# Keeping the last two tiles of each image in SBUF until their coefficients are known, instead of the last one

## What is computed

```python
g = _gn(x)                                   # group norm, 32 groups of 8 channels, no affine part
s = 0.5 * (abs(dx(g)) + abs(dy(g))) + 0.5 * abs(g)      # [-1,0,1] differences, zero padding
sp = mean of s over each 32 x 32 patch       # (4, 256, 64 patches)
ranks = argsort(argsort(-sp, axis=1), axis=1)
mask = ranks < 128                           # in each patch the 128 strongest of 256 channels
return x + g * mask
```

## Time and profile before

| | |
|---|---|
| median of 3 runs | 2076.13 us (2074.24 to 2077.39) |
| the profiled execution: its time | 2073.52 us |
| its span, first to last instruction | 2071.8 us |
| mean granted TensorE clock | 0.829 |
| busy share of the span | VectorE 76%, ScalarE 74%, TensorE 66%, GpSimd 64% |
| DMA traffic | 776.53 MB, mean 375 GB/s |
| HBM read and written | 507.51 MB and 268.44 MB |
| chain that ended last, largest shares | DMA 51%, ScalarE 15%, issue 10%, TensorE 8%, VectorE 8% |

### The profile page before, as it was taken

The page is one execution under the profiler, slowest core; times in us unless marked ns, Lnnn a source line. Parts: engine busy times, 40 slices in busy tenths (PEclk is TensorE's granted clock), DMA queues, the critical chain, the costliest instruction groups (busy, mean ns, idle before and its releaser), DMA issues.

```text
span 2071.8 us, 16156 instructions
## 1 busy us (share of the span) xinstructions
PE 1373.3 (66%) x3528; PEld 673.3 (33%) x3528; DVE 1571.7 (76%) x2160; ACT 1538.2 (74%) x2357; POOL 1321.6 (64%) x894
## 2 busy tenths in 40 slices
PE   5899899786787778676777778776777778300000
PEld 2444444343333334333333334333333334100000
DVE  7988888888777877799778887988778787861322
ACT  4999999897889888998798889997798889400000
POOL 7999899587677766578676667677676667300000
PEclk9999999888888888888888888898988888655555
DMA  6744555199999999999999999999999999699999
GB/s 251 337 183 199 206 243 213 61 369 433 430 429 432 432 434 428 388 370 434 426 431 431 434 429 432 394 395 424 429 432 432 434 428 378 289 420 430 432 430 389
DMA packets 41239, 776.53 MB, mean 375 GB/s; under 512 B 4576, under 2 KB 4576, under 8 KB 4576
## 3 DMA queue, kind: packets, MB, share of 16 engines
q1 hardware_dynamic: 41184, 775.96, 88.5%
HBM read 507.51 MB, written 268.44 MB: 375 GB/s over the span
## 4 chain that ended last, share of the span: by engine, by line
DMA 51%; ACT 15%; issue 10%; PE 8%; DVE 8%; DVEq 2%; POOL 2%; SPq 1%; ACTq 1%; POOLq 0%
DMA again<-in_x_dram 40%; ACT again L653 8%; DMA out_dram<-ring 7%; PE vertical L557 4%; DMA ring<-in_x_dram 4%; PE vertical L559 3%; ACT thrown L705 3%; DVE stats L742 3%; DVEq L733 2%; ACT vertical L699 2%; DVE largest L935 1%; DVE ring L994 1%; SPq L404 1%; DVE vertical L756 1%; ACT pair L693 1%
## 5 line engine op out<-in xcount | busy, mean ns | idle before, releaser
L557 PE MATMUL vertical<-ring,plus 128*128 128x512 f32 (+1 forms) x1200 | 666.8, 640 | 305.6 <-ACT vertical L699 305.3
L273 POOL TENSOR_TENSOR pair<-ring 128x960 f32<-128x960 f32 x360 | 638.7, 1795 | 30.5 <-DVE scratch L913 21.9
L559 PE MATMUL vertical<-ring,minus 128*128 128x512 f32 (+1 forms) x1200 | 633.1, 611 | 0.0
L742 DVE BATCH_NORM_STATS2 stats<-ring 128x6 f32<-128x512 f32 x960 | 582.4, 678 | 24.2 <-DMA ring<-in_x_dram 12.8
L705 ACT ACTIVATE thrown<-ring,record 128x1024 bf16<-128x1024 f32 x480 | 548.1, 1142 | 8.8
L653 ACT ACTIVATE again<-again,coef 128x1024 f32<-128x1024 f32 x360 | 416.1, 1227 | 166.4 <-DMA again<-in_x_dram 166.4
L769 DVE TENSOR_REDUCE sums<-pair 128x2 f32<-128x1920 f32 (+1 forms) x212 | 455.0, 2146 | 83.7 <-POOL pair L273 83.1
L279 POOL TENSOR_TENSOR pair<-ring 128x960 f32<-128x960 f32 x120 | 269.5, 2246 | 296.1 <-DVE sums L769 272.2
L557 PEld LDWEIGHTS vertical<-ring,plus 128*128 128x128 f32 x1200 | 240.6, 212 | 578.3 <-ACT vertical L699 364.5
L559 PEld LDWEIGHTS vertical<-ring,minus 128*128 128x128 f32 x1200 | 250.2, 208 | 296.6 <-issue 296.6
L699 ACT ACTIVATE vertical<-vertical 128x960 f32<-128x960 f32 x320 | 303.5, 949 | 25.0 <-PE vertical L559 25.0
(11 more groups left out here) (103 smaller groups left out, 1117.2 us busy)
## 6 DMA issues: line engine op xcount, KB each, us to landing
ring<-in_x_dram SPq DMA_DIRECT2D x66, 4096.0 KB, 23.3
again<-in_x_dram SPq DMA_DIRECT2D x94, 2048.0 KB, 15.2
out_dram<-again SPq DMA_DIRECT2D x94, 2048.0 KB, 14.4
out_dram<-ring SPq DMA_DIRECT2D x10, 4096.0 KB, 39.0
kept<-in_x_dram SPq DMA_DIRECT2D x7, 4096.0 KB, 23.5
out_dram<-kept SPq DMA_DIRECT2D x8, 2048.0 KB, 9.7
out_dram<-kept SPq DMA_DIRECT2D x3, 4096.0 KB, 33.4
ring<-in_x_dram SPq DMA_DIRECT2D x4, 1024.0 KB, 7.9
```

What stands on the lines that cost most here:

```text
L273: return nc.gpsimd.tensor_tensor(part.rearrange("p (r c) -> p r c", r=PATCH), xs[:, w, :, 2:], xs[:, w, :, 0:PATCH - 2], ALU.subtract)
L557: nc.tensor.matmul(v[:, first:end], plus[:], xs[:, first + 2 * PATCH:end + 2 * PATCH], start=True, stop=False)
L559: done = nc.tensor.matmul(v[:, first:end], minus[:], xs[:, first:end], start=False, stop=True)
L742: nc.vector.bn_stats(stats[:, k, :], buffer[:, k * BN:(k + 1) * BN])
```

## The change

Tile 14 (in `ring[2]`) is now kept like tile 15. `RETAINED` lists both, and `HALVES` is 28: tiles 0 to 13. ScalarE finishes the two halves of tile 14 in tile 0 of the next image, where it finished those of tile 15, and tile 15's halves in tile 1 (`ORDER_BEHIND`: the two `o` of `ORDER` are `k`). The halves loaded again begin in tile 2: `OUT_FIRST` is (0, 0, 2). Tiles 2 to 13 have two each, tile 14 has one, tile 15 one (a new `o` at the head of `ORDER_LAST`), and two follow during the ranking as before. SyncE stores both halves of `ring[2]`, waits until these stores have landed, and only then loads tile 2 into `ring[2]`; the two stores of `kept` come behind the load of tile 3.

```diff
-HALVES = 2 * LAST
+RETAINED = (LAST - 1, LAST)
+HALVES = 2 * (TILES - len(RETAINED))
...
-OUT_FIRST, OUT_LOOPED, OUT_LAST, OUT_RANKING = (0, 2, 2), (2, 2, 2), (2, 2, 2, 0), 2
+OUT_FIRST, OUT_LOOPED, OUT_LAST, OUT_RANKING = (0,0,2), (2, 2, 2), (2,2,1,1), 2
...
-ORDER_LAST = "a0 v0 a1 v1 d a2 a3 v2 a4 a5 v3 a6 a7 v4".split()
+ORDER_LAST = "o a0 v0 a1 v1 d a2 a3 v2 a4 a5 v3 a6 a7 v4".split()
+ORDER_BEHIND = [one.replace("o", "k") for one in ORDER]
...
+            def store_retained(image, n, buffer, signal):
+                for h in range(2):
+                    sp.wait_ge(applied, PER_IMAGE * image - PER_IMAGE + 2 * n + h + 1)
+                    store_half(TILES * image - TILES + RETAINED[n], h, buffer[:, h * HALF:(h + 1) * HALF], signal)
+
             def image_loads(image, last):
                 first, looped, end, ranking = plan
-                load_ahead(image, 0, 0)
-                for h in range(2):
-                    sp.wait_ge(applied, PER_IMAGE * image - PER_IMAGE + h + 1)
-                    store_half(TILES * image - 1, h, kept[:, h * HALF:(h + 1) * HALF], kept_stored)
-                for u in range(RING):
-                    if u:
-                        load_ahead(image, 0, u)
-                    finish_halves(image, 0, first[u])
+                store_retained(image, 0, ring[2], retained_stored)
+                sp.wait_ge(retained_stored, 32 * image)
+                load_tile(TILES * image + 2, ring[2], ring_loaded[2])
+                load_ahead(image, 0, 1)
+                store_retained(image, 1, kept, kept_stored)
+                load_ahead(image, 0, 2)
+                finish_halves(image, 0, first[2])
...
-                for u in range(RING):
-                    sums_of(image, u, ring[u], u, ORDER if u else ORDER_AFTER_RANKING, 0, first[u])
+                sums_of(image, 0, ring[0], 0, ORDER_AFTER_RANKING, retained=((0, 0), (0, 1)))
+                sums_of(image, 1, ring[1], 1, ORDER_BEHIND, retained=((1, 0), (1, 1)))
+                sums_of(image, 2, ring[2], 2, ORDER, 0, first[2])
```

More of the change, by code:

```diff
@@ L162, in groupnorm_patch_topk @@
         kept_stored = sem("kept_stored")
+        retained_stored = sem("retained_stored")
         stats_ready = sem("stats_ready")
@@ L206, in groupnorm_patch_topk @@
         plan = output_plan()
+        uses = [len(range(slot, HALVES, SLOTS)) for slot in range(SLOTS)]
         def by_patch(buffer):
@@ L423, in load_ahead @@
                         load_tile(tile + 2, ring[b], ring_loaded[b])
-                elif peeled and g == 0 and u == 0:
-                    wait_done_with(tile - 1)
-                    load_tile(tile + 2, ring[2], ring_loaded[2])
                 else:
@@ L431, in load_again @@
             def load_again(image, g, w, ahead=0):
[L432 to L435, removed]
+                slot = w % SLOTS
+                sp.wait_ge(again_stored[slot],
+                           16 * (uses[slot] * image + 2 * g + (uses[slot] * (ahead - 1) + w // SLOTS)) + CREDIT_STORED)
+                load_half(TILES * image + RING * g + (TILES * (ahead - 1) + w // 2), w % 2, slot)
             def load_first_again(image):
@@ L442, in finish_halves @@
                 for w in halves:
-                    sp.wait_ge(applied, PER_IMAGE * image + 2 * RING * g + (w + 3 - PER_IMAGE))
+                    sp.wait_ge(applied, PER_IMAGE * image + 2 * RING * g + (w + 1 - HALVES))
                     store_half(TILES * (image - 1) + (RING * g + w // 2), w % 2, again[w % SLOTS][:],
@@ L522, in _ @@
                 sp.wait_ge(again_stored[slot],
-                           16 * (2 * LOOPED * (IMAGES - 1) + (2 if slot == 0 else 1)) + CREDIT_STORED)
+                           16 * (uses[slot] * (IMAGES - 1) + (2 if slot == 0 else 1)) + CREDIT_STORED)
             sp.wait_ge(kept_stored, 32 * (IMAGES - 1) + 16 + CREDIT_STORED)
@@ L656, in apply, with apply_retained, sums_of @@
                 done.then_inc(applied, 1)
-            def apply_kept(image, half):
-                if half == 0:
+            def apply_retained(image, n, half):
+                if n == half == 0:
                     act.wait_ge(coef_ready, image)
-                apply(kept[:, half * HALF:(half + 1) * HALF], LAST, half * HALF_COLS)
+                buffer = (ring[2], kept)[n]
+                apply(buffer[:, half * HALF:(half + 1) * HALF], RETAINED[n], half * HALF_COLS)
             def apply_again(image, g, w):
[L664 to L668, removed]
+                slot = w % SLOTS
+                act.wait_ge(again_loaded[slot], 16 * (uses[slot] * image - uses[slot] + 2 * g + w // SLOTS + 1))
+                apply(again[slot][:], RING * g + w // 2, w % 2 * HALF_COLS)
+            def sums_of(image, t, buffer, r, steps, g=0, halves=(), retained=()):
                 tile = TILES * image + t
                 halves = list(halves)
-                kept_halves = [0, 1] if "k" in steps else []
+                retained = list(retained)
                 assert steps[-1] == f"v{PE_PATCHES - 1}"
@@ L707, in sums_of @@
                     elif kind == "k":
-                        apply_kept(image, kept_halves.pop(0))
+                        apply_retained(image, *retained.pop(0))
                     elif halves:
                         apply_again(image, g, halves.pop(0))
-                assert not halves and not kept_halves
+                assert not halves and not retained
             act.wait_ge(constants, CONSTANTS)
@@ L1003, in _ @@
                 finish(order[n], buffers[n][:])
-            loads = 2 * LOOPED * (IMAGES - 1)
             for q in range(SLOTS):
-                dve.wait_ge(again_loaded[q], 16 * (loads + 1))
+                dve.wait_ge(again_loaded[q], 16 * (uses[q] * (IMAGES - 1) + 1))
                 finish(q // 2, again[q][:], q % 2 * HALF_COLS, HALF_COLS)
@@ L1015, in _ @@
                 finish(n + 2, buffers[n % BUFFERS][:])
-            dve.wait_ge(again_loaded[0], 16 * (loads + 2))
+            dve.wait_ge(again_loaded[0], 16 * (uses[0] * (IMAGES - 1) + 2))
             finish(SLOTS // 2, again[0][:], SLOTS % 2 * HALF_COLS, HALF_COLS)
```

## The result

The change makes the kernel slower: 2102.39 us in the median (2100.86 to 2104.28) beside 2076.60 us for the kernel before, a ratio of 1.0127 with a 95% interval of 1.0115 to 1.0139. That is +26 us where +20.6 us were forecast, and 2102 us where 2097 us were.

A forecast was written before the change was run, and what follows sets the result against it. Inside an image the DMA queue was taken as the limit, behind image ends not. Added queue gaps less 29.3 us of removed transfers gave +20.6 us on the profiled 2073.5, as a median 2097 us; forecast 2084 to 2110, range 2062 to 2113.

The forecast's parts named there:

- What bounds the kernel: Inside an image the DMA queue is the limit, 430 GB/s and 29.3 us a tile; behind an image's end not.
- What is removed: Two halves fewer loaded again at each of three image ends: 12.6 MB, 9.8 us an end, 29.3 us in all.
- The late load: Tile 2 waits for tile 14's stores, so VectorE stalls 21.7, 15.7 and 19.7 us at image ends, 57 us in all.
- The gaps of the queue: Idle queue time around tile 2's late load at an image end: 19.5 us for image 2, against 4.8 before.
- The sum: Gaps less earlier idle time and removed transfers: +8.6, +4.9 and +7.1 us for images 1 to 3, +20.6 us.
- the stall would be absorbed: Rival: engines catch up after the image-end stall and the saved transfers count; faster, 2050 to 2071 us, chance 0.18.
- the engines' delay stays in full: Rival: delay from image ends isn't worked off, removed transfers give nothing; 2130 us, top of 2110 to 2130, chance 0.13.
- half of the delay worked off: Milder form of the rival that the engines' image-end delay stays: about 2103 us, meeting the forecast; no chance of its own.

The follow-up runs named there:

- late_load_alone: Kernel before, with tile 2's load behind the stores of kept and waiting until they land; 30 halves still loaded again: 2101.05 us, 1.0124.
- no_late_load: The change with tile 2's load where it stood before, tile 14 of images 0 to 2 left out of the output: 2063.77 us, 0.9944.
- the combined kernel: The change with tile 14 multiplied sooner, tile 2 loaded in halves, old halves plan for tiles 14 and 15, some VectorE sums before tile 2's statistics: 2064.14 us.
- tile3_first: The change with tile 3's load issued ahead of tile 2's, same transfers: 2134.64 us, 1.0286.
- load_in_halves: The change with tile 2 loaded in two halves, each once the store of its half of ring[2] has landed: 2097.73 us, 1.0105.

## Why the prediction was right, and where it was short

The direction, the place and the size of the stalls were right. That the total came within 5 us is in part luck, because two terms were too large and cancelled. My sum holds 20.6 + 29.3 = 50 us for the late load and takes 29.3 us off for the removed transfers. The runs give 26 us for the late load with nothing taken off (late_load_alone beside before and the change), or 38 us with 11 taken off (by way of no_late_load).

- **What bounds the kernel**: right. Loads of halves still come one a tile, 23 to 24 us each, inside an image, and the slices stand at 430 GB/s.
- **What is removed**: right in bytes (494.93 MB against 494.9), wrong in worth. I put 9.8 us an end, full queue time. Without the late load it is 11 us over three ends, under 4 us each, and with it nothing. Before late_load_alone ran I still priced the kernel with a late load and 30 halves at 2110 us or more, and it ran at 2101.
- **The late load**: right. Stalls of 21.7, 15.7 and 19.7 us were forecast, 21.9, 15.5 and 21.7 measured. In image 2 two small misses cancel: store and load took 7.2 and 12.2 us in the chain against 8.6 and 12.4, but the second store went out 14.3 us behind the coefficients (879.07 to 893.36) and not 13.1. The figures of the Trainium skill ("DMA: Bandwidth & Descriptors", Anatomy of one DMA) are for DMAs of the gpsimd path; as an estimate for these of SyncE they give 6.8 and 11.6 us, which is nearer for this store and 0.6 us low for the load. The third stall was forecast 2.0 us short. VectorE's start at 1353.34 before already had a wait of 1.55 us for tile 2's load in it, which I took for the time at which tile 2 was wanted; the rest is ScalarE, which begins to multiply tile 14 4.4 us behind the coefficients and not 3.8.
- **The gaps of the queue**: right in sum, wrong in kind. For image 2 I laid out 19.5 us against 4.8 before, and the windows show 19.0 against 4.8. But tile 4 is issued 21.0 us behind tile 2's landing (933.88) and not 25.3, so its gap is 1.9 and not 5.2 us; and the hole ahead of tile 2's second store, which goes out at 43.6 (956.45) and not 41.3 us behind the landing into a queue that ran dry the sooner, is 5.7 us and more, not 1.3.
- **The sum**: 5 us short. Between coefficients the images take 477.4, 477.5 and 474.6 us, against 478, 474 and 471 forecast (469.0, 468.8 and 464.4 before). The first is right; the second and third are 3.5 us short each. I priced every transfer at 430 GB/s. In the window around the image end the busy queue moves 340 / 0.84 = 405 GB/s in the change and 400 / 0.96 = 417 before, which over 0.84 x 119 = 100 us is 3 us. The size fits, but no run shows this as the cause. The like window of no_late_load has 382 / 0.94 = 406, so a late load isn't needed for the lower rate. Some of it can be half 27, for which ScalarE waits 1.6 us in the ranking of image 1; putting it back brought 1.5 us between the medians over all three ends, which isn't told from nothing.
- **The rivals**: that the stall would be absorbed was wrong for the change, and right for the combined kernel, once VectorE's order let it be. That the engines' delay stays in full was wrong too (26 us of time for steps 51 us longer). But its form with half of the delay worked off had 2103 us, and it said that the removed transfers then give nothing. This is what late_load_alone shows. So that account fits both kernels with a late load, where my sum fits the change alone. For what comes on top, the full form holds: tile3_first added 33 us of steps and 32 us of time.

## What to carry to other kernels

Keeping data in a buffer saves a transfer, but it makes the next user of that buffer wait for multiply, store and load in a row (9 + 7 + 12 us here), and that lands where the queue is emptiest, so compare the landing with the time at which the next user is needed, before counting the bytes saved. Look at what is queued behind such a wait on the waiting engine: here the cure was to move an engine's own work, and with it the buffers it frees, ahead of the wait, as far as its sources are ready, and no further; which of the two, the work or the freed buffers, brings the gain wasn't tried apart. And a transfer removed from a full queue is worth its time only if the engines can move up into it; beside an image end 9.8 us of it were worth 4 and, with the engines late, nothing.

## What the runs showed of the hardware that I had not expected

A 2 MB store into an idle queue took 7.0 us and the second of a pair 8.6 us in the kernel before, but 6.3 and 7.2 us in the change at the end of image 1. A load of half a tile took far longer than the 4.9 + 2.1 us that I had worked out from the stores: in load_in_halves the second half landed 9.7 us after its issue at the end of image 0 and 10.1 us at the end of image 2, and the first half 10.2 and 11.3 us. Tile 3's load is issued 0.8 and 0.4 us behind the second half, so it may be that a transfer shares the queue with the one issued behind it; a whole tile in the same place, with tile 3 as close behind, took 12.2 us (900.68). So the edit made tile 2 only 1.5 to 3.5 us earlier, which fits its gain of 5 us. The cause of the long landings wasn't tried by itself.

The rows of these single transfers in load_in_halves, first and second half at the end of image 0 and then at that of image 2, and in the change, tile 2 and tile 14's two halves at the end of image 1 (KB, us to landing):

```profile
ring<-in_x_dram SPq DMA_DIRECT2D x1, 2048.0 KB, 10.2
ring<-in_x_dram SPq DMA_DIRECT2D x1, 2048.0 KB, 9.7
...
ring<-in_x_dram SPq DMA_DIRECT2D x1, 2048.0 KB, 11.3
ring<-in_x_dram SPq DMA_DIRECT2D x1, 2048.0 KB, 10.1
```

```profile
ring<-in_x_dram SPq DMA_DIRECT2D x1, 4096.0 KB, 12.2
...
out_dram<-ring SPq DMA_DIRECT2D x1, 2048.0 KB, 6.3
out_dram<-ring SPq DMA_DIRECT2D x1, 2048.0 KB, 7.2
```
